# Attention of a transformer block in another order: weights, copies and transposes moved between and along the queues

## What is computed

```python
x = x + xattn(layernorm(x), ctx_512, Wq, Wkv_expand, Wout)
x = x + ffn(layernorm(x), gate, gate_up, down, shared_gate_up, shared_down)

# xattn, 16 heads of 32
qp = q @ Wq.T
k, v = jnp.split(latent_kv @ Wkv_expand.T, 2, axis=-1)
scores = jnp.einsum('bhqd,bhkd->bhqk', qh, kh) * inv_sqrt_d
causal = jnp.tril(jnp.ones((sq, sk), dtype=bool))
scores = jnp.where(causal, scores, jnp.finfo(scores.dtype).min)
attn = jax.nn.softmax(scores, axis=-1)
out = jnp.einsum('bhqk,bhkd->bhqd', attn, vh)   # then @ Wout.T

# ffn
scores = jax.nn.softmax(x @ gate_weight.T, axis=-1)
topk_w, topk_idx = jax.lax.top_k(scores, 2)
y = sum over the two experts of  (silu(gate) * up) @ down, weighted
y = y + (silu(sgu[:, :Fs]) * sgu[:, Fs:]) @ shared_down.T
```

## Time and profile before

| | |
|---|---|
| median of 3 runs | 379.26 us (378.74 to 381.44) |
| profiled execution | 379.04 us, span 377.1 us |
| mean TensorE clock granted | 0.975 |
| PE busy | 347.1 us (92% of the span) |
| DVE, ACT, POOL busy | 256.4, 237.4, 90.3 us |

### The profile page before, as it was taken

How to read it: one execution, slowest core, us unless ns; L and a number is a source line. 1 busy time by engine, 2 the same in 40 slices (tenths; PEclk the granted TensorE clock), 3 DMA queues, 4 the chain that set the end, 5 groups by cost and what they waited for, 6 DMA issues and landing times.

```text
span 377.1 us, 6793 instructions
## 1 busy us (share of the span) xinstructions
PE 347.1 (92%) x2199; PEld 282.9 (75%) x2200; DVE 256.4 (68%) x461; ACT 237.4 (63%) x617; POOL 90.3 (24%) x106
## 2 busy tenths in 40 slices
PE   6699896988889999999999989999999999999972
PEld 5478783866667677798988778788788788788750
DVE  2983817488886634883767898877877877877820
ACT  3532987899998514221322488788788788788730
POOL 4556110133333000025610001131131131131131
PEclk9899897899999999999999999999999999999997
DMA  7999000000000078999388754435435435435333
GB/s 232 365 368 346 7 0 2 0 3 2 0 3 3 17 318 272 369 421 335 122 263 212 232 194 105 92 56 83 85 56 83 83 56 84 84 56 83 56 34 49
DMA packets 28377, 49.32 MB, mean 131 GB/s; under 512 B 6656, under 2 KB 11776, under 8 KB 27328
## 3 DMA queue, kind: packets, MB, share of 16 engines
q1 hardware_dynamic: 24208, 39.78, 31.8%
q0 software_dynamic: 4144, 9.23, 14.1%
HBM read 32.08 MB, written 16.92 MB: 130 GB/s over the span
## 4 chain that ended last, share of the span: by engine, by line
PE 73%; ACT 9%; DVE 7%; DMA 5%; issue 3%; POOL 1%; POOLq 0%; SPq 0%; ACTq 0%; DVEq 0%
PE bank L488 32%; PE bank L760 21%; PE bank L775 9%; ACT prob L862 6%; PE bank L652 3%; DMA out<-y_sb,dest 3%; PE bank L677 2%; PE bank L663 2%; PE bank L782 2%; DMA w_kv<-wkvT 2%; DVE negmax L1112 1%; DMA w_sg<-sguT 1%; PE bank L480 1%; PE bank L539 1%; DVE bn L1054 1%
## 5 line engine op out<-in xcount | busy, mean ns | idle before, releaser
L1067 DVE TENSOR_TENSOR gu_lo<-w_gu,gu_hi 128x704 fp32r<-128x704 f32 x84 | 72.6, 887 | 19.4 <-ACT gu_hi L816 18.0
L816 ACT ACTIVATE gu_hi<-w_gu 128x704 fp32r x84 | 66.1, 791 | 12.1 <-PE bank L760 11.8
L469 POOL DMA_INDIRECT out<-y_sb,dest x21 | 33.1, 1574 | 148.8 <-ACT y_sb L1009 144.6
L760 PE MATMUL bank<-gu_lo,xsT_hi 128*128 128x352 f32 x168 | 42.8, 336 | 1.0 <-DVE gu_lo L1067 0.8
L760 PE MATMUL bank<-gu_hi,xsT_hi 128*128 128x352 f32 x168 | 40.7, 323 | 0.0
L760 PE MATMUL bank<-gu_hi,xsT_lo 128*128 128x352 f32 x168 | 40.7, 323 | 0.0
L775 PE MATMUL bank<-w_dn,actT_plain 128*128 (+1 forms) x84 | 39.6, 592 | 0.0
L816 ACT ACTIVATE act_s_hi<-act_s 128x512 fp32r<-128x512 f32 (+3 forms) x12 | 6.9, 578 | 43.2 <-DVE act_s L1213 22.7
L488 PE MATMUL bank<-x2T_hi,w_sg_lo 128*128 128x512 f32 (+1 forms) x88 | 32.2, 366 | 0.1
L488 PE MATMUL bank<-x2T_hi,w_sg_hi 128*128 128x512 f32 (+1 forms) x88 | 32.0, 363 | 0.0
L488 PE MATMUL bank<-x2T_lo,w_sg_hi 128*128 128x512 f32 (+1 forms) x88 | 31.9, 362 | 0.0
(11 more groups left out here) (183 smaller groups left out, 789.8 us busy)
## 6 DMA issues: line engine op xcount, KB each, us to landing
w_gu<-guT SPq DMA_DIRECT2D x8, 1408.0 KB
xs_dram<-xs_in SPq DMA_DIRECT2D x1, 5460.0 KB, 20.1
xs_in<-xs_dram SPq DMA_DIRECT2D x21, 256.0 KB, 2.6
w_dn<-dnT SPq DMA_DIRECT2D x8, 512.0 KB, 5.1
w_sg<-sguT SPq DMA_DIRECT2D x10, 256.0 KB
xres<-x SPq DMA_DIRECT2D x2, 768.0 KB, 9.5
w_dn<-dnT SPq DMA_DIRECT2D x8, 192.0 KB, 5.6
w_sd<-sdnT SPq DMA_DIRECT2D x5, 256.0 KB, 5.7
```

Of the source, the lines that this page charges most:

```text
L469: pool.indirect_dma_start(out=out[:, :], out_offset=bass.IndirectOffsetOnAxis(ap=dest[:, i, 0:1], axis=0), in_=y_sb[i % 2][:, :], in_offse ...
L760: ins = pe.matmul(dst[:, 0:F], xsT[x_][:, c, :], gu2[w_][:, c, f0:f0 + F], start=c == 0 and n == 0, stop=c == C - 1 and n == 2)
L816: act.activation(dst, src, ACT.Copy).then_inc(s[sem], 1)
L1067: dve.tensor_tensor(lo_, src, hi_.bitcast(F32), ALU.subtract).then_inc(s[sem], 1)
```

## The change

It puts instructions elsewhere on the queues and gives some to another engine; what is computed, and the number and shape of the instructions, stay the same but for the engine.

- The DMAs of shared weight block 0 (`load_sg(0)`, `load_sd(0)`) are issued ahead of those of `w_o` and `w_gate`. Their splitting moves from the end of iteration 0 to the start: on ScalarE between the query copies, on VectorE before the first maxima.
- The first copy of v (`put_v(0)`) stands before the exponentials of batch 0; the copies of kT and qT of block 0 of the second half stand between these exponentials. On TensorE `scores(0)` goes ahead of `k_proj(1, 0)`.
- In iterations 0 to 2 the copies of the next qT and kT go from ScalarE to VectorE, behind the four maxima. The copies of v in iterations 0 and 1 go to VectorE too, behind `oT_lo`.
- `t2(b-3)` moves from the head of the iteration to behind AV; `put_x2T` and `x2T_lo` move behind `put_oT` and `oT_lo`. In the last iteration the first half of `shared_gu` goes behind the transposes of group 0.

The diff:

```diff
--- before.py
+++ after.py
@@ -260,8 +260,6 @@
             sp.dma_start(w_q[:, :, :], wqT.rearrange("(c p) d -> p c d", p=P)).then_inc(s["wq"], 16)
             sp.dma_start(xres[:, BLK:NX, :], tiles_of(x_rows, BLK, NX)).then_inc(s["xrest"], 16)
             load_ctx(1)
-            sp.dma_start(w_o[:, :, :], woT.rearrange("(c p) d -> p c d", p=P)).then_inc(s["wo"], 16)
-            sp.dma_start(w_gate[:, :, :], gateT).then_inc(s["wgate"], 16)
 
             def load_sg(j):
 
@@ -274,9 +272,12 @@
                 k, w = FSK[j]
                 sp.dma_start(w_sd[SD_BUF[j]][0:w, :], sdnT[k:k + w, :]).then_inc(s[f"wsd{SD_BUF[j]}"], 16)
 
-            for j in range(2):
-                load_sg(j)
-                load_sd(j)
+            load_sg(0)
+            load_sd(0)
+            sp.dma_start(w_o[:, :, :], woT.rearrange("(c p) d -> p c d", p=P)).then_inc(s["wo"], 16)
+            sp.dma_start(w_gate[:, :, :], gateT).then_inc(s["wgate"], 16)
+            load_sg(1)
+            load_sd(1)
             sp.wait_ge(s["zt"], 2)
             sp.dma_start(xs_dram[:, :].rearrange("(n p) d -> p n d", p=P),
                          no_row[:, :].unsqueeze(1).to_broadcast([P, NT, XW])).then_inc(s["zero"], 16)
@@ -587,12 +588,12 @@
             pe.wait_ge(s["wkv_lo2"], 1)
             pe.wait_ge(s["QT"], C - 1)
             v_proj(0)
+            pe.wait_ge(s["xnT_hi"], NX)
+            pe.wait_ge(s["xnT_lo"], NX)
+            scores(0)
             pe.wait_ge(s["ctx_hi"], 2)
             pe.wait_ge(s["ctx_lo"], 2)
             k_proj(1, 0, CC)
-            pe.wait_ge(s["xnT_hi"], NX)
-            pe.wait_ge(s["xnT_lo"], NX)
-            scores(0)
             q_proj(1, 0, D)
 
             def fill(j):
@@ -613,18 +614,15 @@
                 if b + 1 < NB:
                     pe.wait_ge(s["mask"], R * (b + 1))
                     scores(b + 1)
-                else:
-                    pe.wait_ge(s["mask"], R * NB)
-                    pe.wait_ge(s["x2T_hi"], BLK)
-                    pe.wait_ge(s["x2T_lo"], BLK)
-                    shared_gu(0, 0, (0,))
                 if 1 <= b < C - 1:
                     fill_next(b)
-                if b >= 3:
-                    t2(b - 3)
-
 
                 for r in range(R):
+                    if r == 1 and b == NB - 1:
+                        pe.wait_ge(s["mask"], R * NB)
+                        pe.wait_ge(s["x2T_hi"], BLK)
+                        pe.wait_ge(s["x2T_lo"], BLK)
+                        shared_gu(0, 0, (0,))
                     if r == 2 and b == 0:
                         fill_next(0)
                     if r == 1 and b >= 2:
@@ -643,9 +641,9 @@
                         pe.wait_ge(s["prob3"], (R - RP) * b + r - RP + 1)
                     if r == 0:
                         pe.wait_ge(s["Vs"], b + 1)
-                    if r == 1 and b >= 3:
-                        pe.wait_ge(s["x2T_hi"], b - 2)
-                        pe.wait_ge(s["x2T_lo"], b - 2)
+                    if r == 1 and b >= 4:
+                        pe.wait_ge(s["x2T_hi"], b - 3)
+                        pe.wait_ge(s["x2T_lo"], b - 3)
                     if r >= 2:
                         pe.wait_ge(s["probT"], R * b + r - 1)
                     for c in range(C):
@@ -663,9 +661,13 @@
                     ins = pe.matmul(CC[HD * r:HD * (r + 1), c * SQ:(c + 1) * SQ], v_sb[:, h * HD:(h + 1) * HD],
                                     probT[r][:, c, :], start=True, stop=True)
                 ins.then_inc(s["O"], 1)
+                if b >= 3:
+                    t2(b - 3)
                 if b + 1 < NB:
                     v_proj(b + 1)
             shared_gu(0, 0, (1,))
+            pe.wait_ge(s["x2T_hi"], NX - 2)
+            pe.wait_ge(s["x2T_lo"], NX - 2)
             t2(NX - 2)
             pe.wait_ge(s["x1"], NX - 1)
             out_proj(NX - 1, 0, 3 * C)
@@ -895,17 +897,18 @@
                 put_qT(0, j, bank[4 + j])
                 if BLK + j < NX:
                     put_xnT(BLK + j, S[j])
+                if j == 1:
+                    sg_hi(0)
+                if j == 2:
+                    sd_hi(0)
+            put_v(0)
             for r in range(R):
                 exps(0, r)
-            put_v(0)
-            put_kT(1, 0, CC)
-            put_qT(1, 0, D)
+                if r == 0:
+                    put_kT(1, 0, CC)
+                if r == 2:
+                    put_qT(1, 0, D)
             for b in range(NB):
-                if 1 <= b < C - 1:
-                    put_qT(1, b + 1, D)
-                    put_kT(1, b + 1, CC)
-                if b >= 3:
-                    put_x2T(b - 3)
                 if b == 2:
                     act.wait_ge(s["wgate"], 16)
                     hi(w_gate2[0][:, :, :], w_gate[:, :, :], "wg_hi")
@@ -914,9 +917,6 @@
                     put_pT(b, 1)
                 if b + 1 < NB:
                     exps(b + 1, 0)
-                if b == 0:
-                    put_qT(1, 1, D)
-                    put_kT(1, 1, CC)
                 for r in range(2 if b == 0 else 1, R):
                     put_pT(b, r)
                 if b + 1 < NB:
@@ -926,13 +926,13 @@
                     sd_hi(1)
                 act.wait_ge(s["O"], b + 1)
                 put_oT(b)
+                if b >= 3:
+                    put_x2T(b - 3)
                 if b + 1 < NB:
-                    put_v(b + 1)
+                    if b >= 2:
+                        put_v(b + 1)
                     exps(b + 1, 2)
                     exps(b + 1, 3)
-                if b == 0:
-                    sg_hi(0)
-                    sd_hi(0)
 
             def shared_silu(j, t):
                 w = FSK[j][1]
@@ -1122,6 +1122,18 @@
                    .then_inc(s["prob"], 1)
 
             whole = slice(None)
+
+            def put_qT(j):
+                dve.wait_ge(s["Q"], C + j + 1)
+                dve.tensor_scalar(qT[:, j, XC[1]], D[:, 0:WX[1]], SCALE, None, ALU.mult).then_inc(s["QT"], 1)
+
+            def put_kT(j):
+                dve.wait_ge(s["K"], C + j + 1)
+                dve.tensor_copy(kT[1][:, j, :], CC[:, 0:W]).then_inc(s["KT"], 1)
+
+            def put_v(n):
+                dve.wait_ge(s["V"], n + 1)
+                dve.tensor_copy(v_sb[:, :], A[0:SQ, :]).then_inc(s["Vs"], 1)
 
             def oT_lo(b):
                 dve.wait_ge(s["oT_hi"], b + 1)
@@ -1169,6 +1181,8 @@
                 if n > BLK:
                     xnT_lo(n - 1, S[n - 1 - BLK])
             xnT_lo(NX - 1, S[NX - 1 - BLK])
+            sg_lo(0)
+            sd_lo(0)
             for r in range(R):
                 masked(0, r)
             for r in range(R):
@@ -1177,8 +1191,9 @@
                 for r in range(R):
                     if b + 1 < NB:
                         masked(b + 1, r)
-                    if b >= 4 and r == 0 or b == 3 and r == 1:
-                        x2T_lo(b - 3)
+                if b < C - 1:
+                    put_qT(b + 1)
+                    put_kT(b + 1)
                 if b == 2:
                     lo(w_gate2, w_gate[:, :, :], "wg_hi", 1, "wg_lo", (whole, whole, whole))
                 if b >= 2:
@@ -1189,12 +1204,13 @@
                 if b >= 2:
                     apply2(b - 2)
                 oT_lo(b)
+                if b >= 3:
+                    x2T_lo(b - 3)
                 if b + 1 < NB:
+                    if b < 2:
+                        put_v(b + 1)
                     normalised(b + 1, 2)
                     normalised(b + 1, 3)
-                if b == 0:
-                    sg_lo(0)
-                    sd_lo(0)
                 if b == NB - 1:
                     sg_lo(1)
                     sd_lo(1)
```

## The result

The changed kernel is slower: median 382.64 us (380.27 to 386.05, 20 runs), against 379.32 us (376.3 to 381.73, 20 runs) for the kernel before on the same chips. The ratio is 1.0089, 95% interval 1.0063 to 1.0114. The forecast was 377.3 us with a range of 374.6 to 380.8. The profiled execution took 383.16 us (span 381.4, granted clock 0.971); the one of before 379.04 (span 377.1).

A forecast was written before the change was run, and what follows sets the result against it. ScalarE was taken nearly to set the steady period (9.0 of 9.49 us busy). Gains of 5.7 us less 2.4 lost gave 375.7 at full clock, plus 1.6 for one slow stretch: 377.3 us, range 374.6 to 380.8.

The forecast's parts named there:

- Item 7, last iteration: Last iteration: TensorE waits 0.6 us for v and 1.7 for x2T_lo, tile 4's x2T_lo costs 0.1; 2.4 us lost.
- My list: TensorE idle times that might precede a clock fall: 1.5, 1.4, 2.7, and 0.6 with 1.7 us.
- Item 6, steady iterations: Iterations 4 to 6 gain nothing: 0.45 us of ScalarE idle off, 0.4 of waiting added; period 9.45 for 9.49.
- Item 6, iteration 3: Iteration 3 loses a 1.04 us wait for x2T_lo and a 0.5 x2n wait: 0.6 to 0.7 us more gained.
- The clock, one stretch: One half-clock stretch on TensorE's path, taken for the 2.7 us wait, adds 1.6 us; bounds nothing to three stretches, 5.1.
- items 2 and 5: TensorE's waits for VectorE's copies: 1.5 us for kT before iteration 0's AV, 2.7 for qT before iteration 2's output projection.
- Items 1, 2, 5: Start 0.5 us earlier; first AV ends 2.4 earlier despite its kT wait; the qT wait leaves 4.7 of 6.8 gained.
- The cost there is nothing: Start: splitting the first shared weights fits in idle holes, 2.12 us on ScalarE and 4.04 on VectorE.
- A VectorE copy of 0.5: Each kT or qT copy out of PSUM on VectorE takes 0.5 us, judged from rows of 0.59 and 0.60.
- all given back: Case, chance 0.15: three slow stretches, or copies of 0.8 instead of 0.5 us, give 379.2 to 382 us.
- The slower case: Chance 0.05: three waits for VectorE each put TensorE into a long half-clock stretch, 3.4 us lost apiece: 385.9 us.

The follow-up runs named there:

- the two experiments on the copies: From the kernel with the transposes back: kT and qT copies back on ScalarE, 374.86 us (0.9866); or on VectorE between second and third maxima, 374.51 us (0.9876).
- the filler's kernel: The kernel with the transposes back, plus twenty transposes whose result nobody reads in TensorE's wait for qT before the first output projection: 378.26 us, 0.9978.
- the last one: Kernel with copies between the maxima and ScalarE's v copies and exponentials reordered (0.979), with every copy of v moved to VectorE: 374.58 us, 0.9858.

## Why the prediction was wrong

The mechanisms of the early part were right, and the gain is real: without the move it is 0.5%, or 1.8 us. The forecast had 5.0 us of gain by the start of iteration 3, before the moved transposes come in, at full clock, and one slow stretch against it. In the profile of that kernel two slow stretches take 3.3 us of it. That its 1.8 us lie near the 2.0 forecast for the whole is luck, since it leaves out the part that lost. The sum failed in these terms.

- **Item 7, last iteration, -2.4.** Its two waits were found, 0.78 and 1.49 for 0.6 and 1.7. But the term was mis-sized: the stretch lost 3.3 us at full clock and 4.8 in the profiled execution with its half clock. Of the 3.3 (the move alone), waits are 2.4, and 0.4 is t2 of tile 3, which now falls behind the AV of iteration 6. The last 0.5 is what overlap loses at a wait: ahead of two of the three waits the last product counts to its own end, 0.39 us instead of the 0.23 after which the next one starts elsewhere, and ahead of the third four transposes count 0.57 instead of 0.31. My list named this wait as one before which the clock may fall, at 1.7 us, but the one stretch that I took was the qT wait's; the half clock here comes on top.
- **Item 6, steady iterations, "Taken off is what ScalarE idled before".** Wrong. I exchanged 0.48 of x2T_hi for 0.4 of waiting and then struck ScalarE's idle 0.5 as well. That idle time was its wait for the last probT (0.32) and for v (0.18), and neither hung on x2T: the first is there after as well. The new wait of 0.33 came on top: 9.86 for 9.45, 0.4 us in each of three periods.
- **Item 6, iteration 3, +0.6 to 0.7.** It gained 0.1 (2.2 us ahead at its start, 2.3 at its end), as waits of 0.66 for oT_lo and 0.71 for probT took the place of the one removed.
- **The clock, one stretch.** Two on TensorE's path in the kernel without the move, 1.6 to 1.7 us each, behind the waits of items 2 and 5 that I had named. The reason given for taking one, that the 2.7 us wait was longer than the 1.8 that had preceded a fall, was the failing step. It left out the first wait, which I had at 1.5: it was 1.85, and the clock fell. In the changed kernel's profile it fell behind 1.22 us (at 58.8).
- **Items 1, 2, 5.** First scores 0.3 earlier instead of 0.5; AV's wait 0.87 in the changed kernel and 1.83 to 1.86 in its relatives, forecast 1.5; qT's wait 1.62 and 2.3, forecast 2.7. Right in kind and nearly in size. "The cost there is nothing" for the early splits held. w_o was in time by two errors that cancel: it was issued at 13.26 instead of the 10.1 of the forecast, since the issues ahead of it began 0.9 later and that of w_sd took 3.33 us instead of 1.30, but it landed 7.7 us later and not 13.4, at 21.0.
- **A VectorE copy of 0.5.** Right, from start to start. In the changed kernel kT's copy lasts 0.61 us on VectorE and 0.54 on ScalarE for the same 128x448, and the next instruction starts 0.53 and 0.44 us behind its start. The Trainium skill's "Perfetto Trace Analysis" ("Optimizing Scalar/DVE Operations") puts VectorE's access to PSUM, in the time that the engine is busy with it, at some 0.07 us above ScalarE's. The 0.09 from start to start is near that, but no run here separates the access from the rest of the copy. As the two experiments on the copies show, it is not what they cost.

Of the rivals, "all given back" names a time near the result (379.2 to 382). The profiled execution does have its three slow stretches, but only the last stands behind a wait that it counts, and the copies did not take 0.8. The slower case had the right sign and the wrong mechanism: no wait for VectorE was followed by seven us at half clock. The largest loss came from the moved transposes. Items 6 and 7 have them at 1.7 us lost; against the kernel without the move they cost 5.2.

## What to carry to other kernels

When a copy moves from before an engine's wait to behind it, look for which work had covered the wait, and keep the engine's other waits in the sum until the row that releases each is shown to move. What feeds a later stage (here x2T of tile 3 for the shared half) has a due time of its own: made later, it can lose more behind the loop than in all of the loop's turns. Place a copy in a queue by who waits for it: between two maxima or behind four was worth some 3 us, the choice of engine nothing that could be measured.

## What the runs showed of the hardware

The granted clock fell from 1.00 to 0.50 (2.4 to 1.2 GHz) behind idle times of 1.2 to 2.8 us, but not each time in the same part of the program. Behind the wait of 2.3 us for qT it fell in all six kernels that show this wait. Behind the wait of 1.8 us ahead of the first AV it fell in seven of nine; the filler's kernel and the one with the move kept in iterations 3 to 5 stayed at 1.00. Behind the wait of 1.2 us for probT in iteration 1 it fell within a microsecond in four of the fourteen kernels that show this wait, and behind the steady iterations' waits of up to 1.2 us in none. In two kernels it fell with no idle time of note just ahead, at 38.5 us in the changed kernel and at 37 in the last one, both times right behind the first scores, 32 small products on which it was busy for 2.5 us; why there in two kernels and not in the other twelve with that order stays open. So the clock of one profile is not the clock of its kernel, and where the clock fell explains a profiled execution better than it does a median.
